# AdaLN block with routed experts: the final pass over all tokens is folded into the loop over expert tiles

## The reference, cut to what matters

```python
h = layernorm(x) * (1 + ca) + sa
x = x + ga * attention(h)                          # x: 4096 x 256
h = layernorm(x) * (1 + cb) + sb
scores = sigmoid(h @ gate_w + bias)                # 8 experts, the best 2 of each token
w = the 2 best scores, divided by their sum
combined = sum over the 2 experts of w_e * 0.1 * (gelu(h @ up_w[e] + up_b[e]) @ down_w[e] + down_b[e])
shared = (gelu(h @ sw_up + sb_up) @ sw_down + sb_down) * 0.1
out = shared + combined
out = out / (max(abs(out), axis=-1) + 1e-6)        # needs both experts' parts of a token
x = x + gb * out
```

## Time and profile before

| what | value |
|---|---|
| median of three runs | 1032.31 us |
| the profiled execution, its own time | 1029.6 us |
| its span (first to last instruction) | 1028.0 us |
| mean granted TensorE clock | 0.923 |
| PE busy | 858.6 us, 84% |
| weight loads of PE | 788.2 us, 77% |
| DVE busy | 575.8 us, 56% |
| ACT busy | 448.6 us, 44% |
| POOL busy | 319.5 us, 31% |
| DMA | 61.04 MB, mean 59 GB/s |

### The profile page before, as it was taken

One profiled execution on the slowest core, in us unless ns is written; L12 is line 12 of the kernel. 1 busy time (PEld: TensorE's weight loads), 2 busy tenths in 40 slices (PEclk: granted clock), 3 DMA queues, 4 the chain that ended last, 5 costly groups with the idle time before them and its releaser, 6 DMA issues. The chain is left out here.

```text
span 1028.0 us, 21379 instructions
## 1 busy us (share of the span) xinstructions
PE 858.6 (84%) x5989; PEld 788.2 (77%) x5990; DVE 575.8 (56%) x1402; ACT 448.6 (44%) x811; POOL 319.5 (31%) x310
## 2 busy tenths in 40 slices
PE   6899997479999989998659999999999999999000
PEld 4787786468878878777649999989999999999000
DVE  5687874568778768776824343443343333343057
ACT  4665552134543543554435545545554445553000
POOL 3626201113243143243302332333333333333224
PEclk9999999579999989999869999999999999999555
DMA  8020000001011011011561224222232222222153
GB/s 296 24 82 1 1 1 1 0 1 52 14 65 59 6 66 53 11 64 64 181 225 34 45 46 119 42 42 42 44 52 46 42 42 42 42 42 37 22 204 122
DMA packets 41494, 61.04 MB, mean 59 GB/s; under 512 B 6784, under 2 KB 33376, under 8 KB 41312
## 3 DMA queue, kind: packets, MB, share of 16 engines
q1 hardware_dynamic: 25376, 36.50, 10.8%
q0 software_dynamic: 13952, 18.39, 10.5%
q10 hardware_dynamic: 2112, 5.51, 1.4%
HBM read 31.81 MB, written 28.57 MB: 59 GB/s over the span
## 5 line engine op out<-in xcount | busy, mean ns | idle before, releaser
L1601 PE MATMUL psUp<-eT,wup 128*128 128x256 f32 x1632 | 207.1, 287 | 12.0 <-issue 8.3
L1601 PEld LDWEIGHTS psUp<-eT,wup 128*128 128x128 f32 x1632 | 200.5, 194 | 18.0 <-issue 17.3
L1621 PE MATMUL psE<-wdn,gTh 128*128 128x256 f32 x1088 | 197.6, 284 | 0.0
L1667 ACT ACTIVATE gu<-psUp,ubias 128x256 f32<-128x256 f32 x272 | 113.9, 470 | 190.7 <-PE psUp L1601 171.7
L1706 DVE TENSOR_TENSOR gTl<-gu,gTh 128x512 fp32r<-128x512 f32 x136 | 91.5, 691 | 155.4 <-ACT gTh L1672 102.6
L1621 PEld LDWEIGHTS psE<-wdn,gTh 128*128 128x128 f32 x1088 | 167.8, 190 | 0.0
L1755 POOL DMA_INDIRECT ffn_out<-yb,meta x68 | 110.3, 1622 | 171.9 <-DMA ffn_out<-yb,meta 97.8
L1621 PE MATMUL psE<-wdn,gTl 128*128 128x256 f32 x544 | 153.0, 281 | 0.0
L1023 PE MATMUL psU<-h2T,su 128*128 128x512 f32 x384 | 107.0, 416 | 6.6 <-ACT gf L1105 6.6
L1621 PEld LDWEIGHTS psE<-wdn,gTl 128*128 128x128 f32 x544 | 103.6, 190 | 0.0
L1035 PE MATMUL psY<-sd,ghi 128*128 128x256 f32 x512 | 95.0, 285 | 0.8 <-DVE glo L1233 0.8
(11 more groups left out here) (252 smaller groups left out, 1255.7 us busy)
## 6 DMA issues: line engine op xcount, KB each, us to landing
hin<-expert_in SPq DMA_DIRECT2D x36, 256.0 KB, 2.8
X<-in_L_attn_x SPq DMA_DIRECT2D x8, 512.0 KB, 7.3
acc<-ffn_out SPq DMA_DIRECT2D x8, 512.0 KB, 5.1
out<-X ACTq DMA_DIRECT2D x8, 512.0 KB, 2.6
ffn_out<-sh SPq DMA_DIRECT2D x7, 512.0 KB, 3.0
raw_up<-in_L_ffn_up_w SPq DMA_DIRECT2D x3, 1024.0 KB, 5.4
raw_dn<-in_L_ffn_down_w SPq DMA_DIRECT2D x3, 1024.0 KB, 9.4
expert_in<-prow SPq DMA_DIRECT2D x8, 272.0 KB, 7.9
```

What stands on the lines that cost most here:

```text
L1601: mm = nc.tensor.matmul(psU[:, c, (m % 2) * TR:(m % 2 + 1) * TR], wup[s][:, a, k, m * P:(m + 1) * P], eT[:, u, b, k], start=(n == 0), stop ...
L1621: mm = nc.tensor.matmul(psE[:, u, h * C:(h + 1) * C], (gTh, gTl)[a][:, u, m, h * P:(h + 1) * P], wdn[s][:, b, m], start=(n == 0), stop=(n ...
L1667: nc.scalar.activation(gu[:, c % 2, m], psU[:, c, m * TR:(m + 1) * TR], ACT.Gelu, bias=ubias[:, bass.ds(e * MK + 2 * c + m, 1)]).then_inc( ...
```

## The change

The final block is gone. Each token is met twice by the tile loop, once for each of its experts. At the first visit its weighted row is written to HBM; at the second visit one row of 3 KB per token is read back (shared part, x, the first visit's part), the token is finished in the tile loop, and written to `out`.

- In HBM a new tensor `shared_x_part` has three thirds of 1 KB per token: the shared part, x after attention, and the first visit's row, which is filled with zeros at the start of the second block (eight stores of 512 KB by SP). SP also stores X group by group (eight stores of 512 KB), the last of them at the end of the second block, which waits for it; a store of 128 KB to ffn_out goes.
- Two more iotas in the first block, two more small DVE instructions per group of tokens in the second (L1283 and after the reductions of `place`), one more in the tables. They give each row its targets: its token number plus 65536 and its number of thirds, and the larger of the token's two positions, by which a row knows whether it is the second visit.
- In the tile loop DVE computes the targets of 256 rows (four small instructions), adds the gathered shared and first parts (`bs`), forms the sum (`sm`), takes the largest absolute value, adds, inverts, scales and adds x (`fin`). ACT makes the weighted row for the scatter (`ys`) in place of DVE's yb. POOL scatters it to the third of its token (rows of a second visit are out of bounds and are dropped), waits for it to land, gathers the 3 KB rows of the next tile, waits for fin, scatters fin to `out` (rows of a first visit are dropped). SP loads meta.
- The first 32 tiles are always needed, and `needed` is no longer asked for them on DVE, ACT and POOL. The loop body serves tiles 2 to 29; tiles 30 and 31 stand apart, and tiles 32 to 38 are nested in one another's `needed`. For tile 32 and up the gather isn't made ahead, but at the start of its own tile, and from tile 30 POOL waits at the tile's end until both scatters have landed.

```diff
@@ tiles
         body(0, 0, True, 0)
         body(1, 1, True, 0)
-        with eng.Fori(1, ET // 2) as i:
+        with eng.Fori(1, FULL // 2 - 1) as i:
             body(2 * i, 0, True, i)
             body(2 * i + 1, 1, True, i)
-        body(ET - 1, 0, False, ET // 2)
+        body(FULL - 2, 0, True, FULL // 2 - 1)
+        body(FULL - 1, 1, True, FULL // 2 - 1)
+        with ExitStack() as nest:
+            for j in range(FULL, ET):
+                nest.enter_context(needed(eng, j))
+                body(j, j % 2, j + 1 < ET, j // 2)
@@ SP, second block
+            sp.wait_ge(tb_c, 1)
+            for g in range(NG):
+                sp.dma_start(zero_v[:, TG * g:TG * g + TG, :], ...).then_inc(zero_st, 16)
+            for f in range(NG - 1):
                 sp.wait_ge(sh_ev, 2 * f + 2)
                 sp.dma_start(shd_v[:, bass.ds(TG * f, TG), :], sh[:]).then_inc(sh_st, 16)
+                sp.wait_ge(x_ev, 2 * f + 2)
+                sp.dma_start(xr_v[:, bass.ds(TG * f, TG), :], X[:, bass.ds(TG * f, TG), :]).then_inc(x_st, 16)
...
-            sp.dma_start(shd[N:N + P, :], prow[:, 0:C]).then_inc(end_st, 16)
+            sp.wait_ge(x_ev, 2 * NG)
+            sp.dma_start(xr_v[:, TG * (NG - 1):NT, :], X[:, TG * (NG - 1):NT, :]).then_inc(x_st, 16)
             sp.wait_ge(sh_st, 16 * NG)
+            sp.wait_ge(x_st, 16 * NG)
+            sp.wait_ge(zero_st, 16 * NG)
@@ SP, tile loop (one tile)
+            def tails(j, u):
+                row = entry(sp, rtab, j, E * REG - TR)
+                if later(j, 2):
+                    wait(sp, y_ok, 2 * j - 2)
+                    wait(sp, s_ok, 2 * j - 2)
+                sp.dma_start(meta[:, u], hs[bass.ds(row, TR), C:ROW]...).then_inc(m_in[u], 16)
@@ ACT, tile loop
+            def part_out(j, u, i):
+                e = entry(act, etab, j, E - 1)
+                wait(act, ey_ev, j + 1)
+                if later(j, 2):
+                    wait(act, w_st[u], 32 * i)
+                for h in range(2):
+                    nc.scalar.activation(ys[:, u, h], yc[:, h], ACT.Copy, scale=meta[:, u, h, bass.ds(e + 1, 1)]
+                                         ).then_inc(y_ok, 1)
@@ DVE, tile loop
+            def targets(j, u, i):
+                wait(dve, m_in[u], 16 * i + 16)
+                if later(j, 2):
+                    wait(dve, w_st[u], 32 * i)
+                    wait(dve, o_st[u], 32 * i)
+                tok, third, hi = ...
+                nc.vector.tensor_scalar(own[:], iota_h[:], rowf[:, bass.ds(j, 1)], None, ALU.add).then_inc(ix_c, 1)
+                wait(dve, ix_c, 2 * j + 1)
+                nc.vector.tensor_tensor(sec[:], own[:], hi, ALU.is_equal).then_inc(ix_c, 1)
+                wait(dve, ix_c, 2 * j + 2)
+                nc.vector.scalar_tensor_tensor(widx[:, u], sec[:], float(BIG), third, ALU.mult, ALU.add).then_inc(ix_ok, 1)
+                nc.vector.scalar_tensor_tensor(oidx[:, u], sec[:], -float(BIG), tok, ALU.mult, ALU.add).then_inc(ix_ok, 1)
+            def base(j, u, i):
+                wait(dve, g_in[u], 32 * i + 32)
+                if later(j, 1):
+                    wait(dve, s_ok, 2 * j)
+                nc.vector.tensor_tensor(bs[:], gx[:, u, :, 2 * C:3 * C], gx[:, u, :, 0:C], ALU.add).then_inc(b_ok, 1)
             def result(j, u, i):
                 e = entry(dve, etab, j, E - 1)
+                targets(j, u, i)
+                wait(dve, ey_mm, j + 1)
                 if later(j, 1):
-                    wait(dve, y_ok, j)
-                wait(dve, m_in[u], 16 * i + 16)
-                wait(dve, ey_mm, j + 1)
+                    wait(dve, y_ok, 2 * j)
                 nc.vector.tensor_tensor(yc[:], psE[:, u]..., dbias[:, bass.ds(e, 1), :]..., ALU.add).then_inc(ey_ev, 1)
+                base(j, u, i)
                 wait(dve, ey_ev, j + 1)
-                nc.vector.tensor_tensor(yb[:, u], yc[:], meta[...], ALU.mult).then_inc(y_ok, 1)
+                wait(dve, b_ok, j + 1)
+                if later(j, 1):
+                    wait(dve, f_s, 2 * j)
+                for h in range(2):
+                    nc.vector.scalar_tensor_tensor(sm[:, h], yc[:, h], meta[...], bs[:, h], ALU.mult, ALU.add).then_inc(s_ok, 1)
+                wait(dve, s_ok, 2 * j + 2)
+                nc.vector.tensor_reduce(top[:, 0], sm[:], AX.X, ALU.max, apply_absolute_value=True).then_inc(f_c, 1)
+                wait(dve, f_c, 3 * j + 1)
+                nc.vector.tensor_scalar(top[:, 0], top[:, 0], EPS, None, ALU.add).then_inc(f_c, 1)
+                wait(dve, f_c, 3 * j + 2)
+                nc.vector.reciprocal(top[:, 1], top[:, 0]).then_inc(f_c, 1)
+                wait(dve, f_c, 3 * j + 3)
+                for h in range(2):
+                    nc.vector.scalar_tensor_tensor(fin[:, u, h], sm[:, h], top[:, 1, h:h + 1], gate_fb[:],
+                                                   ALU.mult, ALU.mult).then_inc(f_s, 1)
+                wait(dve, f_s, 2 * j + 2)
+                nc.vector.tensor_tensor(fin[:, u], fin[:, u], gx[:, u, :, C:2 * C], ALU.add).then_inc(f_ok, 1)
@@ POOL, tile loop (in place of the two accumulating DMAs, meta and their waits)
+            def body(j, u, more, i):
+                if isinstance(j, int) and j >= FULL:
+                    gather(j, u, i)
+                wait(pool, ix_ok, 2 * j + 2)
+                wait(pool, y_ok, 2 * j + 2)
+                wait(pool, g_in[u], 32 * i + 32)
+                for h in range(2):
+                    nc.gpsimd.indirect_dma_start(out=sx_third[:, :], ...).then_inc(w_st[u], 16)
+                if not isinstance(j, int) or j + 1 < FULL:
+                    gather(j + 1, 1 - u, i + u)      # waits for m_in, f_ok and w_st
+                wait(pool, f_ok, j + 1)
+                for h in range(2):
+                    nc.gpsimd.indirect_dma_start(out=out[0], ...).then_inc(o_st[u], 16)
+                if isinstance(j, int) and j >= FULL - 2:
+                    wait(pool, w_st[u], 32 * i + 32)
+                    wait(pool, o_st[u], 32 * i + 32)
@@ the fourth block
-    with nc.Block() as block:
...
```

More of the change, by code:

```diff
@@ L204, in adaln_block @@
     ld_w = [sem(f"ld_w{i}") for i in range(3)]
-    x_in = [sem(f"x_in{g}") for g in range(NG)]
+    x_in = [sem(f"x_in{g}") for g in range(5)]
+    x_of = (0, 1, 2, 3, 3, 4, 4, 4)
     (consts, c_silu, c_spread, mod_mm, mod_ok, wt_mm, wa_ok, w_hi1, w_lo1, kb_mm, kb_ok, qb_mm, qb_ok, pool0,
@@ L658, in statistics @@
             def statistics(g):
-                dve.wait_ge(x_in[g], 16)
+                dve.wait_ge(x_in[x_of[g]], 16 * x_of.count(x_of[g]))
                 for n in range(TG * g, TG * g + TG):
@@ L1553, in ahead @@
                     weights(sp, e)
+            def tails(j, u):
[3 more added lines that the diff above has]
+                    wait(sp, s_ok, 2 * j - 2)
+                sp.dma_start(meta[:, u], hs[bass.ds(row, TR), C:ROW].rearrange("(h p) c -> p h c", p=P)
+                             ).then_inc(m_in[u], 16)
+            def body(j, u, more, i):
+                if isinstance(j, int) and j >= FULL:
+                    tails(j, u)
+                if more:
+                    rows(j + 2, u)
+                if not isinstance(j, int) or j + 1 < FULL:
+                    tails(j + 1, 1 - u)
+                if more:
+                    ahead(j + 1)
             sp.wait_ge(scat, 16 * TG * TOPK * NG)
@@ L1559, in _ @@
             rows(1, 1)
+            tails(0, 0)
             sp.dma_start(dbias[:], down_b.partition_broadcast(P)).then_inc(db_in, 16)
             ahead(0)
-            with sp.Fori(1, ETL // 2) as i:
-                with needed(sp, 2 * i - 2):
-                    rows(2 * i, 0)
-                ahead(2 * i - 1)
-                with needed(sp, 2 * i - 1):
-                    rows(2 * i + 1, 1)
-                ahead(2 * i)
+            tiles(sp, body)
         @block.tensor
@@ L1657, in gelu @@
                 e = entry(act, etab, j, E - 1)
-                with needed(act, j):
+                if later(j, FULL) and isinstance(j, int):
+                    with needed(act, j):
+                        chunks(j, u, e)
+                else:
                     chunks(j, u, e)
@@ L1672, in chunks @@
                     nc.scalar.copy(gTh[:, u, 2 * c:2 * c + 2], gu[:, c % 2]).then_inc(eu_hi, 1)
-            def body(j, u, more, i):
-                with needed(act, j):
-                    ahead(j)
-                    if more:
-                        gelu(j + 1, 1 - u)
-                        high(j + 2, u)
+            def part_out(j, u, i):
[6 more added lines that the diff above has]
+                                         ).then_inc(y_ok, 1)
+            def body(j, u, more, i):
+                ahead(j)
+                if more:
+                    gelu(j + 1, 1 - u)
+                    high(j + 2, u)
+                part_out(j, u, i)
             high(0, 0)
@@ L1702, in low_g @@
             def low_g(j, u):
-                with needed(dve, j):
```

(49 more changed lines are left out.)

145 lines of the change are left out of this document (65 added, 80 removed).

## The result

The changed kernel takes 1050.31 us at the median of four runs (1047.47 to 1051.68), the kernel before 1032.62 (1027.41 to 1034.15, four runs on the same chip): the ratio is 1.0177, with an interval of 1.0133 to 1.0220. The change makes the kernel slower by 1.8%. The profiled execution has a span of 1049.9 us, 21.9 more than the one before.

The account below looks back on a forecast made before the run. PE bounds the tile loop before, DVE's 14.0 us cycle after; +5 (start) + 56.3 (loop) - 50.7 (end) = +10.6 us on 1032.3 gives 1043 us, range 1014 to 1067.

Parts of the forecast that it names:

- 9.97 - 1.64 + 4.38 + 1.30: DVE's cycle per tile: 9.97 us before, two table reads less, longer chain after yc, more instructions ahead of yc; 14.0 us.
- The price of a wait: DVE's register waits standing alone: 0.24 us with an address to compute, 0.15 without, against 0.02 inside the instruction.
- lower bound: DVE's cycle in the tile loop if each wait costs only 0.02 us: about 12.0 us, PE staying the bound.
- DVE hides under PE: Rival, tile loop: waits overlap with execution, cycle stays 12.3 us, time 987 us; chance 0.22 including a partial share.
- The loop: yc of tile 0 to yc of tile 31: 31 tiles at 14.0 us plus the split, +56.3 us.
- The split tile: Tile where weights are split, in the tile loop: the split lies bare on DVE after the change, 4.7 us.
- The start: Before the tile loop: +3 us for SP's stores ending the second block, +2 for small DVE instructions; +5.
- the iotas: Two more early in the first block: 0, since POOL then waits for DVE's statistics; without that cover 0.4 us.
- The end: yc of tile 31 to the end: 95.8 us before, 45.1 after, through tiles 32 and 33; -50.7 us.
- one more branch and the exit: Last step of the end: from the last scatter's landing at 43.5 us to 45.1 us after yc of tile 31.
- near the break-even: Rival, tile loop: cycle 13.5 to 13.8 us, time 1032 us; chance 0.18.
- POOL or the gather sets the cycle: Rival, tile loop: indirect DMAs cost 1.55 us each and land in 3.8; cycle 14.7 us, time 1065; chance 0.12.

Follow-up runs that it names:

- The first experiment: Changed kernel with DVE's ten waits on its own earlier instructions put inside the instruction that waits: 1029.16 us, ratio 0.9995 to the kernel before.
- the third group: Changed kernel with waits inside, ktab read in its branch and targets moved into the wait for ACT: ratio 0.9947; with ACT's ktab read in its branch too: 0.9929.
- the first group: Changed kernel with one cut each: waits inside 0.9995, ktab read in its branch 1.0031, targets between gTl 0.9953, reduction to scalings left out 0.9708.
- the four edits: Changed kernel with waits inside, ktab read in its branch, targets moved, gathers of tiles 32 and up one tile ahead: 1027.85 us (0.9889); another chip 1000.75 us (0.9701).

## Why the prediction was right, and where it was off

**The bound and the cycle: right, for the reason given.** DVE on its own 9.97 - 1.64 + 4.38 + 1.30 = 14.0; measured 14.06. From yc to the last add 5.31 was said, 5.46 came (787.35 to 792.81), of which 0.27 is that L1817 took 0.44 us instead of 0.17 in this tile. PE's waits for eT were to be 55 us and are 50.6, its busy share from 600 to 900 us was to be near 87% and is 261.23 of 300. Parts of the chain were then taken out singly and came off the cycle: the lone waits 0.98 us, one table read 0.62, the targets 1.07, the chain behind sm down to PE's 12.33.

**The price of a wait: right as it stood, wrong in the lower bound.** The rival *DVE hides under PE* rested on the Trainium skill, VectorE: DVE Perf Modes, section "The DRAIN you can't avoid", where a semaphore behind each Vector instruction cost nothing extra. The first experiment settles it: inside the instruction that is nearly so (0.03 us between reduce and add), standing alone with a register's value it isn't (0.16), and ten of them were 1 us per tile, the whole loss against the kernel before. But the prediction also said that with waits at 0.02 the cycle would be "about 12.0, and PE stays the bound". That was too low: ten waits at 0.13 are 1.3 us, which gives 12.7 from the same rows, and the run with the waits inside measured 13.08. Cheap waits alone don't make the change pay (ratio 0.9995).

**The loop: +57.8 for +56.3.** The near hit is in part luck, errors that cancel. Against 14.0 us per tile, the 27 steady tiles, at 14.12 in the mean, cost 3.2 us more. The split tile lay bare by 6.8 us, not 4.7, since bs waited for the gather beside the weights' load and DVE stood at the split itself:

```profile
684.27 0.69 DVE L1795 TENSOR_TENSOR bs<-gx 128x512 f32<-128x512 f32 x1 [1.43 <-DMA gx<-shared_x_part,meta]
...
691.75 2.36 DVE L902 TENSOR_TENSOR wup<-raw_up,wup 128x1024 fp32r<-128x1024 f32 x2 [2.19 <-issue]
```

On the other side the first distance, where yc still waits for PE, is 11.93 us, and the last two are 12.85 and 13.36: tiles 30 and 31 are written out with constant values for their waits, and from own to yc there are 0.65 us (995.97 to 996.62), where a tile of the loop needs 1.09 (800.12 to 801.21). Together these three save 3.9 us.

**The start: +6.7 for +5.** The second block is 1.0 us longer (+2 was said) and SP ends it 2.4 us later behind ACT than before (+3 was said). And 3.8 us lie in the first block, where I had written 0 for the iotas and not looked at the loads of x that now share semaphores. ACT's last instruction there and in the second block, before and then after:

```profile
L224 ACTq DRAIN  x1: 616/616/616, 169.7 to 169.7; - x1
...
L913 ACTq DRAIN  x1: 273/273/273, 512.2 to 512.2; - x1
```

```profile
L232 ACTq DRAIN  x1: 616/616/616, 173.5 to 173.5; - x1
...
L926 ACTq DRAIN  x1: 158/158/158, 517.0 to 517.0; - x1
```

The twelve kernels with this first block, the changed one among them, had that instruction at 167.8 to 173.6 us, seven of them above 172; 3.8 is near the upper end of a spread, and what makes the spread wasn't tried. Two runs of the third group, whose first blocks are the same program, had 173.3 and 168.3, so it isn't the change's alone. It is there by the time that SP ends its part of the block (60.6 us for 56.7 before). From the second block's end to yc of tile 0 it is 0.5 us less than before.

**The end: -42.5 for -50.7, the term that was mis-sized.** The chain up to the last scatter's landing was nearly exact: the gather of tile 32 was put at 12.3 and 13.6 us after yc of tile 31, and went out at 11.5 and 13.0; that of tile 33 at 28.7 and 30.0, and went out at 28.4 and 29.7.

```profile
1008.11 1.23 POOL L1855 DMA_INDIRECT gx<-shared_x_part,meta  x1 [3.24 <-issue]
1009.64 0.98 POOL L1855 DMA_INDIRECT gx<-shared_x_part,meta  x1 [0.30 <-issue]
...
1025.01 0.99 POOL L1855 DMA_INDIRECT gx<-shared_x_part,meta  x1 [3.28 <-issue]
1026.30 0.98 POOL L1855 DMA_INDIRECT gx<-shared_x_part,meta  x1 [0.30 <-issue]
...
1037.66 0.98 POOL L1873 DMA_INDIRECT out<-fin,oidx  x1 [0.30 <-issue]
```

The waits of bs were longer than I had said (3.7 and 7.6 us for 2.5 and 5), since the gather of 3 KB rows landed 4.7 us after its second issue (1026.30 to 1030.99) and not 3.5, and that was made good by shorter steps elsewhere. POOL's drain starts at 1041.5, 44.8 us after yc of tile 31, where the forecast had the end, at 45.1. The term that was mis-sized is "one more branch and the exit": it was put at 1.6 us behind the last landing and took 9.3 (1040.65 to 1049.9), 8.2 of them the drain, while nothing else runs. In the kernel before POOL's drain behind the same loop took 2.7 us. Together 1.7 + 1.5 + 8.2 = 11.4 us, which is 21.9 - 10.6 but for rounding. The medians of the runs lie 17.7 us apart.

**The rivals.** *DVE hides under PE* fell with the first group, and *near the break-even* with the cycle of 14.06. *POOL or the gather sets the cycle* at 1.55 us per DMA fell as well: the plain indirect DMAs took 0.98 to 1.02 us at the median in all three forms. In its other half it was nearer than the forecast: the gather landed after 4.4 us at the median, where the rival had 3.8 and the forecast 3.5, and yet bs waited for it in only 5 of 34 tiles. Its chain is the next bound.

## What to carry to other kernels

An engine at 39% busy had 2.3 us of 12.3 to spare: before work is moved onto it, lay out its own cycle from a tile in which it was late, with its reads and waits, and price the new chain by the starts of rows like it. Then place the new work where that engine waits for another, and put its waits for itself inside the instructions: form, order and a needless table read, with two gathers ahead, took this kernel from 1.018 to 0.970 of the one before on one chip, to 0.989 on another. And look at the sequencer's rows at the end of every block, since a drain counts as busy nowhere.

## What the runs showed that was not expected

- POOL's drain behind the last indirect DMAs took 8.2 to 8.3 us in the changed kernel and with the four edits, though all their data had landed, and 1.5 us where the scatters to the output were left out. Counted from the start of the last indirect DMA it ended after 12.0, 12.0 and 4.6 us, and in the kernel before after 12.9 (981.8 + 2.7 against 971.59), so it was paid there too: POOL was the last engine at the barrier ahead of the fourth block, PE's drain standing there since 965.2. By that row the end would have been put at 53.9 us behind yc of tile 31 (the last scatter's start at 41.0, and 12.9) and not at 45.1; 53.3 was measured. Why it is short in one kernel isn't settled; no run separates the number of such DMAs from their target.
- One kernel on two chips: the four edits gave 0.9889 on one and 0.9701 on another, while the kernel before differed by 0.8% (1038.14 and 1029.83). A verdict near 1% on one chip wasn't safe for this kernel.
- The same small instruction (L1817, 128x2) took 0.17 us in some tiles and up to 0.45 in others. In the changed kernel it was long in 26 of the loop's 31 tiles, and in each of them it ended within 0.03 us of the end of one of POOL's indirect DMA instructions, as here (791.32 for both):

```profile
790.34 0.98 POOL L1866 DMA_INDIRECT shared_x_part<-ys,widx  x1 [4.90 <-issue]
```

  It adds 5.5 us to the loop. With the waits inside, which shifts the instruction against POOL, it is long in 6 tiles and adds 0.9 us, so a part of that edit's gain is this and not the price of a wait. The reciprocal behind it never took more than 0.17 us, under POOL's instructions or not. What holds the one and not the other isn't shown.
